# Image-prompt cross-attention on one core: third q projection in five matmuls, result rows added by GpSimd, and a new order of norm, statistics and attention's copy

## What is computed

```python
q = split_heads(x @ w_q)                      # 20 heads of 16
k, v = split_heads(text @ w_k), split_heads(text @ w_v)
k_ip, v_ip = split_heads(ip_h @ w_k_ip), split_heads(ip_h @ w_v_ip)
out = merge(softmax(q k^T / 4) v) + merge(softmax(q k_ip^T / 4 + mask_ip) v_ip)
y = out @ w_out + b_out + x
```

## Time and profile before

| | us |
|---|---|
| median of 3 runs | 1300.65 (1300.4 to 1303.57) |
| profiled execution, device time | 1301.75 |
| its span, first to last instruction | 1300.0 |
| TensorE busy | 1179.9 (91%) |
| TensorE weight loads busy | 1120.3 (86%) |
| VectorE busy | 1040.8 (80%) |
| ScalarE busy | 857.4 (66%) |
| GpSimd busy | 760.8 (59%) |

### The profile page before, as it was taken

One profiled execution on the slowest core, in us unless ns is written; L12 is line 12 of the kernel. 1 busy time (PEld: TensorE's weight loads), 2 busy tenths in 40 slices (PEclk: granted clock), 3 DMA queues, 4 the chain that ended last, 5 costly groups with the idle time before them and its releaser, 6 DMA issues.

```text
span 1300.0 us, 34051 instructions
## 1 busy us (share of the span) xinstructions
PE 1179.9 (91%) x12734; PEld 1120.3 (86%) x12734; DVE 1040.8 (80%) x2182; ACT 857.4 (66%) x1795; POOL 760.8 (59%) x876
## 2 busy tenths in 40 slices
PE   6999878489999999999999999999999999999986
PEld 5898878379999998999999999999999999999885
DVE  5688865568888888888888888888888888888883
ACT  2343433467777777777777777777777777777772
POOL 0111110057777777777777777777777777777774
PEclk9999988789999999999999999999999999999998
DMA  6388887655455444454554444444545454555431
GB/s 168 66 190 176 155 155 145 109 108 119 111 114 114 111 111 113 110 118 113 114 111 111 111 111 111 111 111 111 116 115 116 115 116 114 116 111 113 101 73 41
DMA packets 361459, 151.30 MB, mean 116 GB/s; under 512 B 298641, under 2 KB 350865, under 8 KB 360017
## 3 DMA queue, kind: packets, MB, share of 16 engines
q1 hardware_dynamic: 361296, 149.13, 52.0%
HBM read 88.17 MB, written 39.90 MB: 99 GB/s over the span
## 4 chain that ended last, share of the span: by engine, by line
PE 56%; DVE 19%; ACT 9%; issue 6%; SPq 3%; POOL 2%; DMA 1%; DVEq 0%; POOLq 0%
PE ps_a L832 12%; PE ps_b L832 10%; PE ps_s L877 7%; PE ps_o L907 7%; PE ps_s L883 6%; PE ps_m L853 5%; DVE q_hi_lo L1271 4%; DVE heads L1303 4%; DVE aT_lo L1311 4%; ACT aT_hi L1053 3%; ACT prob L1068 3%; PE ps_v L199 3%; PE ps_a L818 2%; PE ps_k L199 2%; DVE inv L1299 2%
## 5 line engine op out<-in xcount | busy, mean ns | idle before, releaser
L1399 POOL TENSOR_TENSOR prob_lo<-prob,prob_hi 128x512 f16<-128x512 f32 (+1 forms) x448 | 486.6, 1099 | 228.5 <-ACT prob_hi L1069 228.3
L1068 ACT ACTIVATE prob<-ps_s 128x512 f32<-128x512 f32 (+1 forms) x448 | 253.3, 565 | 224.4 <-PE ps_s L883 223.9
L877 PE MATMUL ps_s<-q_hi_lo,keys 128*128 128x256 f32 x960 | 262.4, 310 | 6.2 <-DMA q_hi_extra<-q_hi_lo 6.1
L1069 ACT ACTIVATE prob_hi<-ps_s 128x512 f16<-128x512 f32 (+1 forms) x448 | 250.7, 560 | 0.0
L883 PE MATMUL ps_s<-q_hi_extra,keys 128*128 128x256 f32 x960 | 235.5, 282 | 0.0
L1289 DVE TENSOR_REDUCE stats<-ps_m 128x8 f32<-128x552 f32 x320 | 231.0, 722 | 0.0
L907 PE MATMUL ps_o<-values,prob_hi 128*128 128x68 f16 (+7 forms) x3584 | 199.5, 192 | 27.1 <-DVE heads L1303 27.1
L907 PEld LDWEIGHTS ps_o<-values,prob_hi 128*128 128x128 f16 x3584 | 175.3, 98 | 55.5 <-issue 41.1
L907 PE MATMUL ps_o<-values,prob_lo 128*128 128x68 f16 (+3 forms) x1792 | 190.3, 192 | 0.0
L877 PEld LDWEIGHTS ps_s<-q_hi_lo,keys 128*128 128x128 f32 x960 | 172.7, 190 | 6.6 <-DMA q_hi_extra<-q_hi_lo 6.5
L883 PEld LDWEIGHTS ps_s<-q_hi_extra,keys 128*128 128x128 f32 x960 | 173.7, 190 | 0.1
(11 more groups left out here) (179 smaller groups left out, 2916.6 us busy)
## 6 DMA issues: line engine op xcount, KB each, us to landing
x_in<-in_x_dram SPq DMA_DIRECT2D x64, 320.0 KB, 2.9
q_hi_extra<-q_hi_lo SPq DMA_DIRECT2D x64, 320.0 KB, 3.3
x_keep<-in_x_dram SPq DMA_DIRECT2D x64, 320.0 KB, 4.2
out_dram<-y SPq DMA_DIRECT2D x128, 160.0 KB, 2.9
k_scratch<-k_stage SPq DMA_DIRECT2D x16, 770.0 KB, 5.7
keys<-k_scratch SPq DMA_DIRECT2D x256, 48.1 KB, 2.1
ctx_in<-in_ctx_dram SPq DMA_DIRECT2D x64, 128.0 KB, 2.8
keys<-k_scratch SPq DMA_DIRECT2D x256, 24.1 KB, 1.9
```

What stands on the lines that cost most here:

```text
L877: mm(ps, keys[:, n, 0, quad, c:c + P], q_hl[n][:, quad, :], start=i == 0, stop=False)
L1068: nc.scalar.activation(prob[:, s, 0:w], ps_s[(b[1] + s) % 2][:, 0:w], ACT.Exp)
L1069: nc.scalar.activation(prob_hi[par(b)][:, s, 0:w], ps_s[(b[1] + s) % 2][:, 0:w], ACT.Exp).then_inc(s_hi, 1)
L1399: nc.gpsimd.tensor_tensor(prob_lo[par(b)][:, s, 0:w], prob[:, s, 0:w], prob_hi[par(b)][:, s, 0:w], ALU.subtract).then_inc(s_lo, 1)
```

## The change

The last 64 columns of w_q get their high weights in columns 256 to 319 and their low weights in columns 320 to 383 of one tile (`pair_last_columns`, setup). The third projection is then five matmuls of 128 weight columns: high x, low x and the joint tail, each against high and low weights at once. Rows 0 to 63 of the result hold the product with the high weights, rows 64 to 127 that with the low ones, and `q_lo(2)` adds the latter in one more VectorE instruction that waits for the one before.

`finish` moves from VectorE to GpSimd, behind rest(3). As GpSimd takes it from SBUF, ScalarE first copies the rows out of PSUM (`y_out(0)` behind exps 1, `y_out(1)` behind exps 2), and what waited for the result rows to free ps_a and ps_b waits for these copies.

The order: `a_hi` stands ahead of exps 0; `norm(1)` ahead of q_lo 1; norm 0 is no longer followed by finish; `spread_values` 1 and 2 stand behind maxima 2 and behind image_maxima; `stats_transpose` goes to bank 0 of ps_m and stands behind project 1, and the first copy of `extra` behind q_hi 1, ahead of exps 6, the second behind exps 6; the next step's max_scores 0 waits for that first copy.

```diff
@@ TensorE
+                        if m == 2:
+                            terms = [xT[0][:, 0, :], xT[0][:, 1, :], xT[1][:, 0, :], xT[1][:, 1, :], xT2[:, :]]
+                            for i, k in enumerate((0, 1, 0, 1, 2)):
+                                last = mm(ps_a[:, 0:S], wq[0][:, k, 256:384], terms[i], start=i == 0, stop=i == 4)
+                            last.then_inc(s_q, 1)
+                            return
...
                         if h4 == 0:
                             pe.wait_ge(s_keys[third(b)], nth3(b, 16 * NKDMA))
+                            wait(pe, s_ex, b, 2, -1)
...
                         if E:
                             project(e, 0)
                             project(e, 1)
+                        if A:
+                            stats_transpose(a)
                         if Cs:
                             sum_heads(c, 3)
                         if Bs:
                             scores(b, 6)
                         if E:
                             project(e, 2)
-                        if A:
-                            stats_transpose(a, E, Ds)
@@ ScalarE
+                        def y_out(t):
+                            act.wait_ge(s_op, at(d, NT, t + 1))
+                            if t == 0 and (n is None or n >= 4):
+                                act.wait_ge(s_y[par(d)], nth(d, 32, -32))
+                            nc.scalar.copy(y[par(d)][:, t, :], (ps_a, ps_b)[t][:, 0:D]).then_inc(s_ye, 1)
...
-                        if Bs:
-                            exps(0)
                         if Ds:
                             a_hi()
                         if Bs:
+                            exps(0)
                             exps(1)
+                        if Ds:
+                            y_out(0)
+                        if Bs:
                             exps(2)
+                        if Ds:
+                            y_out(1)
+                        if Bs:
                             exps(3)
...
                             q_hi(1)
+                        if A:
+                            extra()
                         if Bs:
                             exps(6)
+                        if A:
+                            extra_quads()
                         if E:
                             q_hi(2)
@@ VectorE
+                            if m == 2:
+                                dve.wait_ge(s_q2, at(e, 1, 1))
+                                nc.vector.tensor_tensor(q_hl[third(e)][QD:P, 4, :], ps_a[QD:P, 0:S],
+                                                        q_hl[third(e)][QD:P, 4, :].bitcast(fp32), ALU.add).then_inc(s_qlo, 1)
...
                             spread_values(0)
-                            spread_values(1)
-                            spread_values(2)
...
-                        if Ds:
-                            finish(0)
                         if A:
                             maxima(2)
-                        if Ds:
-                            finish(1)
+                        if Bs:
+                            spread_values(1)
...
                             image_maxima()
+                        if Bs:
+                            spread_values(2)
                         if E:
                             q_lo(0)
-                            q_lo(1)
                         if Cs:
                             norm(1)
                         if E:
+                            q_lo(1)
                             q_lo(2)
@@ GpSimd
+                        def finish(t):
+                            pool.wait_ge(s_ye, at(d, NT, t + 1))
+                            if t == 0:
+                                pool.wait_ge(s_xb, at(d, 1, 1))
+                            nc.gpsimd.tensor_tensor(y[par(d)][:, t, :], y[par(d)][:, t, :], x_keep[par(d)][:, t, :],
+                                                    ALU.add).then_inc(s_yr, 1)
...
                             rest(3)
+                        if Ds:
+                            finish(0)
+                            finish(1)
+                        if Bs:
                             rest(4)
```

More of the change, by code:

```diff
@@ L548, in xattn_kernel @@
             s_qlo = sem("qT_ready")
+            s_q2 = sem("last_heads_lo_started")
             s_mps = sem("max_scores")
@@ L810, in x_transpose @@
                         if n is None or n >= 2:
-                            pe.wait_ge(s_yr, at(b, NT, -3 * NT))
+                            pe.wait_ge(s_ye, at(b, NT, -3 * NT))
                         else:
                             wait(pe, s_qlo, b, QUADS, 0)
-                            wait(pe, s_ex, b, 2, -2)
                         for t in range(NT):
@@ L840, in project @@
                             pe.wait_ge(s_xlo, at(b, 2, 2))
-                        ps = (ps_a, ps_b, ps_a)[m]
+                        if m == 2:
[4 more added lines that the diff above has]
+                            return
+                        ps = (ps_a, ps_b)[m]
                         split_product(ps[0:KW[m], 0:S], lambda k: xT[0][:, k, :], lambda k: xT[1][:, k, :], xT2[:, :],
@@ L855, in max_scores, with stats_transpose @@
                         last.then_inc(s_mps, 1)
-                    def stats_transpose(b, E, Ds):
+                    def stats_transpose(b):
                         pe.wait_ge(s_ip, at(b, 1, 1))
-                        if E:
-                            pe.wait_ge(s_qlo, at(b, QUADS, QUADS + 4))
-                        elif Ds:
-                            pe.wait_ge(s_yr, at(b, NT, 2 - 3 * NT))
                         for t in range(NT):
-                            last = nc.tensor.transpose(ps_b[:, t * P:(t + 1) * P], stats[:, t, :], ident[:])
+                            last = nc.tensor.transpose(ps_m[:, 0, t * P:(t + 1) * P], stats[:, t, :], ident[:])
                         last.then_inc(s_et, 1)
@@ L910, in sum_heads, with attn_transpose @@
                         last.then_inc(s_pv, 1)
-                    def attn_transpose(b, A, Bs):
-                        if Bs:
-                            pe.wait_ge(s_ex, at(b, 2, 5))
+                    def attn_transpose(b, A):
                         if A:
@@ L918, in attn_transpose @@
                         else:
-                            wait(pe, s_yr, b, NT, 0)
+                            wait(pe, s_ye, b, NT, 0)
                         for t in range(NT):
@@ L946, in step @@
                         if Ds:
-                            attn_transpose(d, A, Bs)
+                            attn_transpose(d, A)
                         if Bs:
@@ L1054, in a_hi, with extra_quads @@
                             nc.scalar.activation(aT2[0:64, :], ps_b[0:64, 0:S], ACT.Copy, scale=f[0:64]).then_inc(s_ahi, 1)
+                        def y_out(t):
[3 more added lines that the diff above has]
+                            nc.scalar.copy(y[par(d)][:, t, :], (ps_a, ps_b)[t][:, 0:D]).then_inc(s_ye, 1)
                         def extra():
                             act.wait_ge(s_et, at(a, 1, 1))
-                            nc.scalar.copy(q_ex[par(a)][QD:P, 0, :], ps_b[QD:P, 0:S]).then_inc(s_ex, 1)
+                            nc.scalar.copy(q_ex[par(a)][QD:P, 0, :], ps_m[QD:P, 0, 0:S]).then_inc(s_ex, 1)
+                        def extra_quads():
                             act.wait_ge(s_ex, at(a, 2, 1))
@@ L1182, in split_main, with pair_last_columns @@
                         then(nc.vector.tensor_tensor(a[1][:], raw[:], a[0][:].bitcast(fp32), ALU.subtract))
+                    def pair_last_columns():
+                        then(nc.vector.tensor_copy(wq[0][:, :, D:384], wq[1][:, :, 256:D].bitcast(fp32)))
                     def make_mask(t):
@@ L1271, in q_lo @@
                                 nc.vector.tensor_tensor(q_hl[third(e)][QD:P, 2 * m + o, :], ps[o * QD:(o + 1) * QD, 0:S],
-                                                        q_hl[third(e)][0:QD, 2 * m + o, :].bitcast(fp32), ALU.subtract).then_inc(s_qlo, 1)
+                                                        q_hl[third(e)][0:QD, 2 * m + o, :].bitcast(fp32), ALU.subtract
+                                                        ).then_inc(s_q2 if m == 2 else s_qlo, 1)
+                            if m == 2:
+                                dve.wait_ge(s_q2, at(e, 1, 1))
+                                nc.vector.tensor_tensor(q_hl[third(e)][QD:P, 4, :], ps_a[QD:P, 0:S],
+                                                        q_hl[third(e)][QD:P, 4, :].bitcast(fp32), ALU.add).then_inc(s_qlo, 1)
                         def maxima(h4):
@@ L1315, in a_lo @@
                                                            in1=aT2[0:64, :].bitcast(fp32), op0=ALU.mult, op1=ALU.subtract).then_inc(s_alo, 1)
-                        def finish(t):
-                            dve.wait_ge(s_op, at(d, NT, t + 1))
-                            if t == 0:
-                                dve.wait_ge(s_xb, at(d, 1, 1))
```

(5 more changed lines are left out.)

7 lines of the change are left out of this document (3 added, 4 removed).

## The result

The changed kernel takes 1321.34 us in the median (1315.62 to 1323.65, 4 runs), the kernel before 1300.66: ratio 1.0155, 95% interval [1.0135, 1.0175]. It is slower by 1.6%; the forecast was 1317. The profiled execution of after is 1322.41 us with a span of 1320.6, 20.66 us above the profiled execution of before.

What follows compares the result with a forecast made beforehand. GpSimd's loop was to bound the step: 0.64 + 2.08 + 12.99 + 0.48 = 16.19 us against 15.98, +12.6 over 60 steps; with +3.2 at the ends, 1301.75 became 1317.6, forecast as 1317, range 1288 to 1346.

Steps and rivals of the forecast that it cites:

- the ends: Outside the 60 complete steps: setup copy taken as zero, +2.3 us in step 62, +0.9 for the last rows; +3.2 together.
- GpSimd's loop: add_heads(1), attn_transpose, a_hi, exps(0), rest(0) and GpSimd's queue set the step: 16.19 us against 15.98; chance 0.5.
- The pause of 2.72: GpSimd between steps: 0.64 us from add_heads(1)'s end to a_hi, then 2.08 from a_hi through exps(0) to rest(0).
- 12.99 + 0.48: GpSimd's own work from rest(0) through add_heads(1), 12.99 us, plus 0.48 for one wide and one narrow spread meeting.
- the next line: VectorE's last q_lo ahead of attn_transpose, forecast to set a step of 15.7 to 15.8 us.
- finish at 0.83: Each of two fp32 128x320 additions moved to GpSimd takes 0.83 us, between 0.76 and 0.88; +1.66 a step.
- The meetings: spread_values beside GpSimd instructions: a wide one costs GpSimd 0.34 or 0.33 us, the narrow 0.14; VectorE 0.5 to 0.6 each.
- The wait at the heads' sums: TensorE's 0.63 us a step, put down to norm(1) running late behind two q_lo, ends with norm(1) ahead of them.
- The last q_lo's line: Third projection's first matmul to attn_transpose: 3.34 us against 2.09 of TensorE work; stall 1.25 to 1.4, step 15.7 to 15.8.
- the sign "waits 1.3 to 1.9 us at attn_transpose and no longer at the heads' sums": Listed as showing the forecast right: TensorE waits 1.3 to 1.9 us at attn_transpose and none at the heads' sums.
- TensorE's own need: TensorE taken alone, without its two waits and the three removed matmuls, could step in about 14.4 us.
- The rule of full blocking: Rival: GpSimd waits out whole spreads, or spread 0 is caught too; step 16.52 to 16.68, 1337 to 1347 us; chance 0.15.

Runs made afterwards that it cites:

- Experiment 1: Changed kernel with one more 128x320 GpSimd addition per step, into a spare tile between the two of finish; one execution 1373.42 us, step 16.99.
- experiment 6: Changed kernel with GpSimd's bias addition moved from behind rest(2) to ahead of rest(0); 1295.81 us, ratio 0.9955 to the kernel before, step 15.78.
- experiment 12: Kernel before the change with only GpSimd's bias addition moved ahead of its first rest; 1409.23 us, ratio 1.083.
- experiment 2: Changed kernel with exps(0) back ahead of a_hi on ScalarE; 1329.93 us, ratio 1.0221 to the kernel before, step 16.34.
- experiment 8: Changed kernel with bias addition ahead of rest(0), q_hi(2) ahead of extra_quads, and first half of q_lo(1) ahead of norm(1); 1295.54 us, ratio 0.9963.
- experiment 9: Changed kernel with finish back on VectorE, reading PSUM, without ScalarE's copies; 1354.92 us, ratio 1.0409 to the kernel before, step 16.81.
- experiment 11: Changed kernel: finish on VectorE without ScalarE's copies, spread 2 behind spread 0, q_hi(2) first, half q_lo(1) ahead of norm(1), bias addition first; 1350.39 us, ratio 1.0386.
- experiment 5: Changed kernel with the three spread_values of a step together again behind maxima 0; 1323.12 us, ratio 1.0169 to the kernel before, step 16.19.
- experiment 3: Changed kernel with q_hi(2) ahead of extra_quads on ScalarE; 1319.69 us, ratio 1.014 to the kernel before, step 16.18.
- experiment 4: Changed kernel with exps(0) ahead of a_hi and q_hi(2) ahead of extra_quads; 1310.77 us, ratio 1.0074 to the kernel before, step 16.06.
- experiment 7: Changed kernel with bias addition ahead of rest(0) and q_hi(2) ahead of extra_quads; 1284.69 us, ratio 0.9878 to the kernel before, mean step 15.68.
- experiment 10: Changed kernel: finish on VectorE without ScalarE's copies, spread 2 behind spread 0, q_hi(2) first, half q_lo(1) ahead of norm(1); 1311.78 us, ratio 1.008.

## Why the prediction was right, and where it was not

The forecast of the time, 1317 against 1321.34, rests on a step that came out to 0.01 us and on ends that came out short: of the 20.66 us, 15.8 were forecast, 12.6 in the steps (measured 11.5) and 3.2 at the ends (measured 9.1).

**GpSimd's loop: right, and shown.** Forecast 16.19 us a step, measured 16.18. The pause of 2.72 was forecast as 0.64 + 2.08 = 2.72; GpSimd's work between was forecast as 12.99 + 0.48 = 13.47, and is 16.18 - 2.72 = 13.46. Experiment 1 shows that no slack is left in it, experiment 6 that 1.5 us taken out of it moves the bound to the next line.

**finish at 0.83: right.** Two take 1.84 us from start to start (1019.29 to 1021.13), with 0.17 for the meeting in it (forecast 0.14). ScalarE's copy takes 0.43 (forecast 0.45).

**The meetings: GpSimd's side right, VectorE's side wrong.** GpSimd lost the 0.33 (L1429, 0.66 instead of 0.33) and the 0.17. For VectorE I had put 0.5 to 0.6 on every spread, as if the price were the spread's. It is 0.26 for the wide one and 0.68 for the narrow one, and up to 1.35 in experiment 12. This did no harm to the forecast, because VectorE was not on the path, which is partly luck: with rest(0) 0.07 us ahead of spread 0, experiment 2 lost 0.3 us a step. It has a part in the misses of experiments 2, 8, 9, 11 and 12.

**The wait at the heads' sums: wrong.** "norm(1) ahead of q_lo(1) and q_lo(2) ends the 0.63 wait": 0.54 is left. VectorE's norm(1) in the changed kernel, and then TensorE from the sum before it to the sum behind it:

```profile
1005.18 0.41 DVE L1325 RECIPROCAL inv<-ps_o 128x40 f32<-128x40 f32 x1
1005.70 0.82 DVE L1329 TENSOR_TENSOR heads<-ps_o,inv 128x640 f32<-128x640 f32 x1
```

```profile
1004.80 0.18 PE L910 MATMUL ps_o<-values,prob_lo 128*128 128x34 f16 x1
...
1005.21 0.51 PE L845 MATMUL ps_a<-xT_hi,wq_hi 128*128 128x256 f32 x2
...
1005.91 0.44 PE L861 MATMUL ps_m<-keys,q_hi_lo 128*128 128x308 f32 x2
1006.67 0.21 PE L910 MATMUL ps_o<-values,prob_hi 128*128 128x51 f16 x2 [0.32 <-DVE heads L1329]
```

The norm starts 0.2 us behind the sum's end and ends at 1006.52; TensorE's other work in the meantime ends at 1006.35. The round trip is longer than its cover, whatever stands behind it on VectorE. In experiments 5 and 6 VectorE even stands idle 0.5 us for the sum (25.0 over 49 and 25.9 over 51), and TensorE's wait is 0.54 as here (26.3 over 49, 26.8 over 50). The three matmuls that the change removes were in that cover, so by these rows their 0.35 us bought nothing at this place; no run puts them back. I had costed the wait as the delay behind q_lo, and not asked how long the round trip is without it.

**The last q_lo's line: right in place and length, but its wait is 0.6 instead of 1.25 to 1.4.** From the third projection's first matmul (1005.21, above) to attn_transpose it is 3.21 us, forecast 3.34:

```profile
1008.42 0.44 PE L925 MATMUL ps_a<-ident,attn 128*128 128x128 f32 x2 [0.39 <-DVE q_hi_lo L1297]
```

Of these TensorE works 2.09 (the prediction's sum) and waits 0.54 at the heads' sums, the wait that I had taken as gone; that leaves 0.58, and 0.60 is measured, with 0.41 for GpSimd behind it. So the sign "waits 1.3 to 1.9 us at attn_transpose and no longer at the heads' sums" came out as 1.01 there and 0.54 at the sums. With GpSimd's loop out of the way the step is 15.78 (experiment 6), within the 15.7 to 15.8 of the prediction: both waits lie in the same stretch of TensorE's queue, so what one had too little the other had too much.

**TensorE's own need: right to 0.25 us.** Forecast about 14.4 us a step. In the changed kernel and in experiments 1 to 11, the step less TensorE's waits is 14.45 to 14.65, and 14.87 in the kernel before, with the three matmuls more.

**The ends: mis-sized.** Forecast +3.2: 0 at the front, +3.2 in the tail. Measured +5.1 and +3.9. At the front the pause ahead of the first complete rest(0) is 3.43 us where it was 1.47, so 2 of the 5.1 are the loop's first turn, which I had counted from step 2 on only. The rest lies earlier, in the steps that fill the pipeline. At rest(0) of the step before the first complete one, after is 1.6 us behind (283.15 against 281.56), and 1.6 more come up to add_heads(1) (295.51 against 292.33), where GpSimd waits 1.0 us for the heads that it did not wait for before. The first 1.6 fall where TensorE's granted clock is at its lower level, 1.2 GHz, for part of the time. Stretches of after (columns as in the earlier trace rows):

```profile
260.00:270.00 10.00, 5.63 (x24) 5.16 (x24) 3.78 (x6) 4.32 (x8) 3.49 (x3) 0.58 0.44 109
270.00:280.00 10.00, 8.16 (x43) 7.72 (x43) 7.68 (x16) 4.90 (x13) 3.48 (x3) 0.66 0.36 83
```

In the kernel before the same two stretches have 0.67 and 0.71. In both kernels TensorE was busy for 0.88 of the 10 us ahead of them. Whether the lower clock causes this part of the delay or follows from it was not tried; from 280 to 310 us the granted clock is 1.00 in both. The 3.9 us of the tail (forecast 3.2) were not taken apart.

**The rule of full blocking.** The case in which GpSimd waits out the whole of a spread was set at up to 16.68 us a step. GpSimd's loop measured 16.18, so its price is the smaller one: 0.33 for a spread of 0.57, 0.17 for one of 0.40. In the other direction VectorE does wait for all that GpSimd's instruction has left (experiments 2, 9, 11 and 12, last section). The section "Who interferes with whom" of the page "SBUF — State Buffer" of the Trainium skill calls this an exclusive lock, in which the later of the two instructions waits for the earlier. VectorE's side agrees with it here; on GpSimd's side the measured price is below the spread's length, and the measurement decides.

## What to carry to other kernels

Before moving an instruction on one engine, list what it will then lie beside on the engine with which it shares a path: the same move of one GpSimd addition gave 2% in one kernel, where GpSimd's queue set the step, and cost 8% in the other, where VectorE had three spreads in that pause and TensorE waited behind them. When a loop through several engines is found, work out the next two as well. Here undoing its cause alone made the kernel slower (experiment 2), undoing it together with the edit of experiment 3, where the spread missed the rest, gave 0.8% (experiment 4), and filling the loop's idle pause with work from inside it gave 1.9% (experiment 6).

## What the runs showed of the hardware

**VectorE's spread_values, whose two inputs both lie in SBUF, waits for GpSimd's running instruction to end.** The wait shows as a longer instruction and not as idle time. The length of a wide spread in the timelines is what GpSimd's instruction has left and about 0.43 us, and never less than the 0.57 that it takes alone:

| kernel | spread starts | GpSimd's instruction ends | left | left + 0.43 | measured |
|---|---|---|---|---|---|
| experiment 6, spread 0 | 1007.09 | 1005.86 + 1.54 | 0.31 | 0.74 | 0.74 |
| after, spread 1 | 1014.55 | 1014.06 + 0.87 | 0.38 | 0.81 | 0.83 |
| experiment 2, spread 0 | 1013.05 | 1012.98 + 1.16 | 1.09 | 1.52 | 1.53 |
| experiment 9, spread 1 | 1009.86 | 1009.69 + 1.17 | 1.00 | 1.43 | 1.43 |
| experiment 11, spread 1 | 1006.73 | 1006.44 + 1.16 | 0.87 | 1.30 | 1.31 |
| experiment 12, spread 0 | 1006.17 | 1006.10 + 1.55 | 1.48 | 1.91 | 1.92 |

For the narrow spread, 0.40 alone, the same holds with 0.26: in after at 1003.16 finish(0) has 0.82 left, and it takes 1.08.

**GpSimd's next instruction pays less than the spread's length:** 0.33 us for a wide spread (L1429 0.66 instead of 0.33 in the changed kernel; 1.49 instead of 1.17 for the rest in experiment 12), 0.37 for the rest that starts just behind one in experiment 4 (1.53 instead of 1.16), and 0.17 for a narrow one. So for VectorE the price is anything from nothing to nearly the partner's whole length, and for GpSimd it is nearly constant. A shift of 0.1 us decides which: a spread that starts just ahead of a rest keeps its own length, and one that starts with it or just behind takes about 1.0 us more (experiments 2 and 4, 7 and 8). In the main part of the kernel before, the tail was the only place where the two met, and its sum over three spreads (3.06 against 1.37) hid this.
